# A late LayerNorm's transposes move into the next unit, and a stage's right operands are made over two units

## The chip, the cores and the metric

The kernel runs on one core of a Trainium2 chip. The metric is the device time of one execution in microseconds (us); the kernel before takes 1109.93 us (median of three runs, 1108.16 to 1110.4). TensorE's multiplications bound it; the other engines prepare their operands and take their results. Below, PE is TensorE, DVE is VectorE, ACT is ScalarE, POOL is GpSimd and SP is the engine that issues most of the DMAs.

## The reference, cut to what matters

2048 tokens of 512 features in fp32 pass through an RWKV-like block (attention part, then a channel mix) and a gated feed-forward block:

```
kk = (h * cm_mk + hh * (1 - cm_mk)) @ Wkey.T        # 512 -> 2048
kv = silu(kk) @ Wval.T                               # 2048 -> 512
sr = sigmoid((h * cm_mr + hh * (1 - cm_mr)) @ Wcr.T)
x  = x + sr * kv
...
x2 = x + attn(layernorm(x))
h  = layernorm(x2)                                   # the last norm
gate, up = split(h @ w_gate_up.T)                    # 512 -> 2 * 2048
out = x2 + (silu(gate) * up) @ w_down.T              # 2048 -> 512
```

h and hh are a normalised token and the one before it. The second norm of the channel mix and the last norm both stand between large products.

## The kernel before, in words

Every fp32 operand of a multiplication is split in two: a high part, rounded to the type in which PE multiplies at full rate (ACT copies it), and a low part, the rest (DVE or POOL subtracts). A product of two operands is three passes: high by high, high by low, low by high.

The last and longest part of the kernel is 48 **units** on PE; in the trace unit 8 begins at 423.3 us, unit 16 at 594.8, unit 32 at 850.2. Units 0 to 15 are key units (the channel mix), units 16 to 47 gate units (the feed-forward). The tokens are four blocks of 512; two blocks make a pair. There are four **stages**: units 0 to 7 (channel mix, first pair), 8 to 15 (channel mix, second pair), 16 to 31 (feed-forward, first pair), 32 to 47 (feed-forward, second pair). Inside a unit a 2x2 block product is made by a scheme with seven products in place of eight (Strassen-Winograd). Its seven left operands (A11 ... S4) come from the unit's weights; the seven right operands (B11, T3, T2, B21, T1, T4, B22) come from the tokens of the pair and are the same for all units of a stage. They lie in `combo`, one buffer for all stages, so an operand of the next stage may be written only after the last unit of the stage before has used it.

A unit on PE (`unit`, from L639): X A11·B11, V S3·T3, tiles of slot 0, Y S2·T2, X A12·B21, tiles of slot 1, Y S1·T1, tiles of slot 2, Z A22·T4, Y S4·B22, tiles of slot 3. X, Y, V and Z are four of the PSUM banks. Each product is six matmuls. The tiles (`out_tile`, six matmuls each) multiply the activated results of the unit before with the second weight matrix; they use the four other PSUM banks, A[0] to A[3], and DVE adds each to `resid` (L1215). A key unit has two tiles in each slot, a gate unit one, unit 17 only two in all.

All engines take their instructions in order, and this order is written out by hand in the function `unit` of each engine. DVE's chain in a unit: `accumulate` of slot 0, `seed` (Z from Y and the copied seventh product, L1266; PE's S1 product waits for it), `sums` (left operands of the next unit, L1161 to L1166, in the fresh units 0 to 7 and 16 to 31), slot 1, `sum_v` (L1270; PE's S4 product waits for it), slot 2, `gate` (L1280, gate units; PE's S3 product of the next unit waits for both), slot 3, and pieces of the last norm. ACT's: copy of X to Y (L890; PE's S2 product waits for it), copy of V (L896), high parts of the gated tiles of the unit before (L845), high parts of the next unit's left operands (L810, L813) and of the second weights (L823), and SiLU of the results as they come (L854, L866).

For the right operands of the next stage, the last unit of a stage has on DVE, in between: `combo_lo_of` (low parts, L1189, two instructions per operand), `make_t2` (L1196), `make_t4` (L1203), and on ACT `combo_hi_of` (high parts, L840, two per operand). T4 is made out of B21 and T2, T2 out of B22 and T1, and T1 and T3 by `right_sums` (L1180, L1183), some units ahead, in units 4, 14 and 30. In the kernel before, all high parts are issued in the last unit of the old stage, and of the low parts T4's and B22's in the first unit of the new one, behind `seed`.

The last norm of block j runs on DVE in seven pieces over some units. The last piece writes normalised tiles (L1241) at the end of unit `NORM3_UNIT[j]` (12, 13, 25 and 29). Right behind slot 3 of the same unit PE transposes them (16 small matmuls, L637) into A[0] to A[3], and ACT copies the four banks back (L879), after which the next unit's first tiles may write them. The copies must wait for all 16 transposes, since they write the buffer that the transposes read.

Of the kernel before, what the change touches and what calls it, by code (L numbers as in the profile page):

```python
# [32 lines left out]
BLOCKS = TOKENS // BT  # L33
# [55 lines left out]
B11, B21, B22, T4, T1, T2, T3 = range(SEVEN)  # L89
# [4 lines left out]
def stage_of(u):  # L94
    return max(n for n in range(STAGE_COUNT) if FIRST[n] <= u)


def stage_start(u):
    return u in FIRST
# [20 lines left out]
def tiles_until(u):  # L120

    if u < KEYS:
        return 2 * SUBS * u
    return SUBS * (u + KEYS - 1) - (LAG if u > KEYS else 0)
# [37 lines left out]
def piece_unit(j, piece):  # L162
    return piece_at(j, piece) // 2

NORM3_UNIT = tuple(piece_unit(j, NORM_PIECES - 1) for j in range(BLOCKS))
NORM3_AFTER = tuple(tiles_until(u) for u in NORM3_UNIT)

SUMS_UNIT = (None, 4, KEYS - 2, FIRST[3] - 2)  # L170

# [29 lines left out]
def build(nc, x, wts, wide, tall, vectors, identity, out):  # L201
# [3 lines left out]
    with ExitStack() as ctx:  # L205
# [270 lines left out]
        def _(pe):  # L476
# [6 lines left out]
            def product(acc, u, a, c, fresh):  # L483

                if stage_start(u):
                    pe.wait_ge(combo_lo, 2 * (SEVEN * stage_of(u) + MADE_ORDER.index(c) + 1))
                wts_of = left[u % 2]
                for k in range(2):
                    hi, lo = (wts_of[:, part, a, k * P:(k + 1) * P] for part in range(2))
                    pe.matmul(acc[:], hi, combo[:, c, k, 0, :], start=fresh and k == 0, stop=False, skip_group_check=True)  # L490
                    pe.matmul(acc[:], hi, combo[:, c, k, 1, :], start=False, stop=False, skip_group_check=True)  # L491
                    mm = pe.matmul(acc[:], lo, combo[:, c, k, 0, :], start=False, stop=k == 1, skip_group_check=True)  # L492
                return mm
# [137 lines left out]
            def norm3(j):  # L631
                pe.wait_ge(z3_ready, SUBS * (j + 1))
                for n in range(NORM3_AFTER[j], NORM3_AFTER[j] + SUBS):
                    s = n % SUBS
                    pe.wait_ge(added, n - SUBS + 1)
                    for k in range(KT):
                        mm = pe.transpose(A[s][:, k * P:(k + 1) * P], fin[j % 2][:, s, k * P:(k + 1) * P], ident[:])  # L637
                    mm.then_inc(t3_psum, 1)

            def unit(u):  # L640
                def some(slot):
                    for n in tiles_in(u, slot):
                        out_tile(n)

                def left_there(part):
                    if u in FRESH:
                        pe.wait_ge(left_lo, 2 * fresh_until(u) + part + 1)
                    else:
                        pe.wait_ge(left_loaded[u % 2][part], 16 * same_parity(CACHED, u))

                left_there(0)
                if u:
                    pe.wait_ge(silu_done, silu_by(u - 1, 0))
                else:
                    pe.wait_ge(sr_ready, SUBS * (BLOCKS - 1) + 1)
                product(X, u, A11, B11, True).then_inc(p1, 1)
                left_there(1)
                if u == 0:
                    pe.wait_ge(sr_ready, SUBS * (BLOCKS - 1) + 3)
                elif is_key(u - 1):  # L660
                    pe.wait_ge(silu_done, silu_by(u - 1, 2))
                else:
                    pe.wait_ge(gated, 2 * (u - KEYS))
                product(V, u, S3, T3, True).then_inc(p7, 1)
                some(0)
                pe.wait_ge(x_copied, u + 1)
                product(Y, u, S2, T2, False).then_inc(p6, 1)
                product(X, u, A12, B21, False).then_inc(p2, 1)
                some(1)
                pe.wait_ge(z_seeded, u + 1)  # L670
                product(Y, u, S1, T1, False).then_inc(p5, 1)
                some(2)
                product(Z, u, A22, T4, False).then_inc(p4, 1)
                pe.wait_ge(v_summed, u + 1)
                product(Y, u, S4, B22, False).then_inc(p3, 1)
                some(3)
                for j in range(BLOCKS):
                    if u == NORM3_UNIT[j]:
                        norm3(j)

            pe.wait_ge(ident_loaded, 16)
            first_norm1()
# [27 lines left out]
        def _(act):  # L710
# [157 lines left out]
            def gated_hi(u):  # L868
                for b in range(2):
                    n = 2 * (u - KEYS) + b  # L870
                    act.wait_ge(gated, n + 1)
                    inner_hi_tile(4 * KEYS + n, 2 * chunk_of(u) + b, u % 2)
# [9 lines left out]
            def unit(u):  # L882

                after = stage_of(u + 1) if u + 1 < UNITS and stage_start(u + 1) else None
                act.wait_ge(p1, u + 1)
                if u:
                    act.wait_ge(silu_done, silu_by(u - 1, 3 if is_key(u - 1) else 1))
                else:
                    act.wait_ge(sr_ready, SUBS * BLOCKS)
                act.activation(Y[:], X[:], ACT.Copy).then_inc(x_copied, 1)  # L890
                if after is not None:
                    combo_hi_of(after, B11)
                act.wait_ge(p7, u + 1)
                if u:
                    act.wait_ge(v_summed, u)
                act.activation(seventh[:], V[:], ACT.Copy).then_inc(seventh_copied, 1)  # L896
                if u > KEYS:
                    gated_hi(u - 1)
                if after is not None:
                    combo_hi_of(after, T3)  # L900
                if u + 1 in FRESH:
                    unit_left_hi(u + 1, 0)
                if is_key(u):
                    unit_right_hi(u)
                if after is not None:
                    combo_hi_of(after, T2)
                if u + 1 in FRESH:
                    unit_left_hi(u + 1, 1)
                act.wait_ge(p2, u + 1)
                if is_key(u):  # L910
                    key_tile(u, 0, X)
                else:
                    gate_tile(u, 0, X)
                    unit_right_hi(u)
                if after is not None:
                    combo_hi_of(after, B21)
                    combo_hi_of(after, T1)
                if is_key(u):
                    act.wait_ge(p4, u + 1)
                    key_tile(u, 1, Z)  # L920
                    act.wait_ge(v_summed, u + 1)
                    key_tile(u, 2, V)
                act.wait_ge(p3, u + 1)
                if is_key(u):
                    key_tile(u, 3, Y)
                else:
                    gate_tile(u, 1, Y)
                if after is not None:
                    combo_hi_of(after, T4)
                    combo_hi_of(after, B22)  # L930
                for j in range(BLOCKS):
                    if u == NORM3_UNIT[j]:
                        norm3(j)

            act.wait_ge(vec_loaded, 16)
            matrix_hi(ITEM_R)
# [46 lines left out]
        def _(dve):  # L983
# [298 lines left out]
            def unit(u):  # L1282

                after = stage_of(u + 1) if u + 1 < UNITS and stage_start(u + 1) else None
                def some(slot):
                    for n in tiles_in(u, slot):
                        accumulate(n)

                some(0)
                if after is not None:  # L1290
                    combo_lo_of(after, B11)
                seed(u)
                if stage_start(u) and u:
                    combo_lo_of(stage_of(u), T4)
                    combo_lo_of(stage_of(u), B22)
                if u + 1 in FRESH:
                    sums(u + 1)
                if is_key(u):
                    last_norm(u, 0)
                some(1)  # L1300
                if after is not None:
                    make_t2(after)
                sum_v(u)
                if after is not None:
                    combo_lo_of(after, T3)
                if u in SUMS_UNIT:
                    right_sums(SUMS_UNIT.index(u))
                some(2)
                if after is not None:
                    combo_lo_of(after, T2)  # L1310
                    combo_lo_of(after, B21)
                if not is_key(u):
                    gate(u, 0)
                    gate(u, 1)
                some(3)
                last_norm(u, 1)
                if after is not None:
                    make_t4(after)
                    combo_lo_of(after, T1)

            first_norm1()
            dve.wait_ge(const_done, 7)
# [232 lines left out]
```

## Time and profile before

| | |
|---|---|
| median of three runs | 1109.93 us (1108.16 to 1110.4) |
| the profiled execution's own time | 1111.04 us |
| its span, first to last instruction | 1109.2 us |
| mean granted TensorE clock | 0.989 of full speed |
| PE busy | 1065.0 us, 96% of the span |
| PE weight loads busy | 875.0 us, 79% |
| DVE busy | 641.9 us, 58% |
| ACT busy | 485.7 us, 44% |
| POOL busy | 542.1 us, 49% |

PE's busy time is made of matmul records that overlap: a matmul of 512 columns shows 0.39 us, and the next begins 0.23 us after the first one's start. Idle time on PE is therefore read from the distance of two starts, and from the bracket with which the timeline marks a wait. The granted clock has two levels, 1.2 GHz (shown as 0.50) and 2.4 GHz (1.00).

### The profile page before, as it was taken

Reading aid. Unit: us, or ns where it says so; the run is one execution under the profiler, and the core shown is the slowest. Engines: PE = TensorE matmul, PEld = TensorE weight load, DVE = VectorE, ACT = ScalarE, POOL = GpSimd, SP = SyncE. Lnnn points to the kernel's source line nnn. Section 1 sums busy time; section 2 is a strip of 40 time slices with the busy share of each in tenths; the row PEclk is TensorE's granted clock in tenths of the full one; section 3 lists DMA queues with packets and bytes.
Section 4 is the critical chain, followed back from the end, with each engine's and each line's share of the span. In section 5 each row is a group of like instructions: output and inputs, shape, how many; then the busy total and the mean of one; then the engine's idle time right before and its main releaser. Section 6 shows DMA issues by size and latency. Waiting matters only on the chain. (4 is left out here: it accounts for less than half of the span.)

```text
span 1109.2 us, 13090 instructions
## 1 busy us (share of the span) xinstructions
PE 1065.0 (96%) x4704; PEld 875.0 (79%) x4704; DVE 641.9 (58%) x1106; ACT 485.7 (44%) x807; POOL 542.1 (49%) x451
## 2 busy tenths in 40 slices
PE   5979999999999999999998999999998999999998
PEld 4758888777788887888786888887876888888887
DVE  7867756685355457465348567676668433333334
ACT  6765676856534435323344433334434222222221
POOL 6483552733766554544435555664554333333322
PEclk9989999999999999999998999999999999999999
DMA  8000222258834444553312466565436454444422
GB/s 306 1 1 1 38 39 76 39 209 255 322 125 150 145 171 122 190 160 109 128 62 105 165 231 192 198 220 190 171 114 218 133 191 141 152 144 150 151 77 76
DMA packets 45233, 157.18 MB, mean 142 GB/s; under 512 B 4080, under 2 KB 4208, under 8 KB 40560
## 3 DMA queue, kind: packets, MB, share of 16 engines
q1 hardware_dynamic: 30000, 108.10, 27.9%
q0 software_dynamic: 15168, 48.24, 14.5%
q8 instruction: 37, 0.61, 0.2%
q14 instruction: 28, 0.23, 0.1%
HBM read 97.60 MB, written 58.72 MB: 141 GB/s over the span
## 5 line engine op out<-in xcount | busy, mean ns | idle before, releaser
L1215 DVE TENSOR_TENSOR resid<-bank,resid 128x512 f32<-128x512 f32 x240 | 164.7, 689 | 244.6 <-PE bank L481 243.0
L490 PE MATMUL bank<-combo,left 128*128 128x512 f32 x672 | 265.1, 395 | 12.7 <-ACT bank L890 7.2
L1447 POOL TENSOR_TENSOR inner<-made,inner 128x512 fp32r<-128x512 f32 x128 | 167.0, 1326 | 220.0 <-ACT inner L845 220.0
L491 PE MATMUL bank<-combo,left 128*128 128x512 f32 x672 | 263.5, 392 | 0.0
L492 PE MATMUL bank<-combo,left 128*128 128x512 f32 x672 | 263.3, 392 | 0.0
L479 PE MATMUL bank<-right,inner 128*128 128x512 f32 x512 | 199.3, 389 | 0.0
L480 PE MATMUL bank<-right,inner 128*128 128x512 f32 x512 | 199.2, 389 | 0.0
L481 PE MATMUL bank<-right,inner 128*128 128x512 f32 x512 | 199.2, 389 | 0.0
L1425 POOL TENSOR_TENSOR left<-quart,left 128x512 fp32r<-128x512 f32 x96 | 116.2, 1232 | 104.8 <-ACT left L810 53.9
L490 PEld LDWEIGHTS bank<-combo,left 128*128 128x128 f32 x672 | 127.3, 190 | 42.7 <-ACT bank L890 8.5
L492 PEld LDWEIGHTS bank<-combo,left 128*128 128x128 f32 x672 | 127.4, 190 | 26.8
L491 PEld LDWEIGHTS bank<-combo,left 128*128 128x128 f32 x672 | 127.5, 190 | 26.1
L1442 POOL TENSOR_TENSOR right<-tall_staged,right 128x512 fp32r<-128x512 f32 x64 | 85.2, 1342 | 56.8 <-ACT right L823 56.8
L479 PEld LDWEIGHTS bank<-right,inner 128*128 128x128 f32 x512 | 96.2, 188 | 20.5 <-POOL inner L1447 0.4
L481 PEld LDWEIGHTS bank<-right,inner 128*128 128x128 f32 x512 | 96.1, 188 | 20.0
L480 PEld LDWEIGHTS bank<-right,inner 128*128 128x128 f32 x512 | 96.1, 188 | 19.9
L1404 POOL TENSOR_TENSOR operand<-made,operand 128x512 fp32r<-128x512 f32 x64 | 84.9, 1425 | 44.2 <-ACT operand L719 44.2
L866 ACT ACTIVATE made<-bank 128x512 f32<-128x512 f32 x64 | 37.9, 593 | 150.7 <-PE bank L492 150.7
L854 ACT ACTIVATE made<-bank 128x512 f32<-128x512 f32 x64 | 37.5, 586 | 95.2 <-PE bank L492 95.2
L845 ACT ACTIVATE inner<-made 128x512 fp32r<-128x512 f32 x128 | 77.2, 628 | 2.7 <-ACT made L854 0.4
L1280 DVE TENSOR_TENSOR made<-bank,made 128x512 f32<-128x512 f32 x64 | 44.0, 690 | 58.5 <-ACT made L866 37.1
L479 PE MATMUL bank<-operand,weights 128*128 128x512 f32 x176 | 69.3, 394 | 1.4 <-DVE made L1128 1.1
(128 smaller groups left out, 1461.7 us busy)
## 6 DMA issues: line engine op xcount, KB each, us to landing
kept_left<-left SPq DMA_DIRECT2D x24, 1792.0 KB, 8.2
left<-kept_left POOLq DMA_DIRECT2D x24, 1024.0 KB, 7.1
left<-kept_left POOLq DMA_DIRECT2D x24, 768.0 KB, 5.1
tall_staged<-tall SPq DMA_DIRECT2D x64, 256.0 KB, 3.6
quart<-wide SPq DMA_DIRECT2D x24, 512.0 KB, 4.2
raw<-kept SPq DMA_DIRECT2D x32, 256.0 KB, 6.3
landed<-wts SPq DMA_DIRECT2D x20, 256.0 KB, 5.8
resid<-x POOLq DMA_DIRECT2D x4, 1024.0 KB, 9.2
```

Source lines behind the costliest of these rows:

```text
L479: pe.matmul(acc, left(0), right(0), start=first, stop=False)
L480: pe.matmul(acc, left(0), right(1), start=False, stop=False)
L481: return pe.matmul(acc, left(1), right(0), start=False, stop=last)
L490: pe.matmul(acc[:], hi, combo[:, c, k, 0, :], start=fresh and k == 0, stop=False, skip_group_check=True)
L491: pe.matmul(acc[:], hi, combo[:, c, k, 1, :], start=False, stop=False, skip_group_check=True)
L492: mm = pe.matmul(acc[:], lo, combo[:, c, k, 0, :], start=False, stop=k == 1, skip_group_check=True)
L845: act.activation(inner[:, h % 4, i, 0, :], made_at(n), ACT.Copy).then_inc(inner_hi, 1)
L1215: dve.tensor_tensor(tile, A[s][:], tile, ALU.add).then_inc(added, 1)
L1404: pool.tensor_tensor(place(kind, b, k, 1), made[:, (n + k) % RING, :], place(kind, b, k, 0).bitcast(F32), ALU.subtract).then_inc(op_lo, 1)
L1425: lo = pool.tensor_tensor(left[u % 2][:, 1, a[0]:a[0] + n, :], quart[:, a[0] + 1:a[0] + 1 + n, :], left[u % 2][:, 0, a[0]:a[0] + n, :].bit ...
L1442: pool.tensor_tensor(right[:, g % 2, i, 1, :], tall_staged[i][:], right[:, g % 2, i, 0, :].bitcast(F32), ALU.subtract).then_inc(right_lo, 1)
L1447: pool.tensor_tensor(inner[:, h % 4, i, 1, :], made_at(n), inner[:, h % 4, i, 0, :].bitcast(F32), ALU.subtract).then_inc(inner_lo, 1)
```

## The change

Two things. First, `NORM3_UNIT` is one unit later (13, 14, 26, 30), and the transposes stand inside that unit, between the products A12·B21 and the tiles of slot 1; `NORM3_AFTER` is the first tile of slot 1, and that tile now waits for the first of ACT's copies. ACT's copies stand behind the copy of V and the gated high parts, ahead of the left operands.

Second, the order of the right operands' work. On DVE `seed` goes ahead of B11's low parts, `sum_v` ahead of `make_t2`; T1's low parts and `make_t4` go to the beginning of the new stage's first unit, ahead of slot 0; B22's low parts go behind `sum_v`; `right_sums` goes from slot 2 to behind slot 3 and the gates. On ACT T4's and B22's high parts go into the first unit of the new stage, behind the copy of V, and T2's goes behind the first SiLU.

```diff
-NORM3_UNIT = tuple(piece_unit(j, NORM_PIECES - 1) for j in range(BLOCKS))
-NORM3_AFTER = tuple(tiles_until(u) for u in NORM3_UNIT)
+NORM3_UNIT = tuple(piece_unit(j, NORM_PIECES - 1) + 1 for j in range(BLOCKS))
+NORM3_AFTER = tuple(tiles_in(u, 1)[0] for u in NORM3_UNIT)
...PE
                 product(X, u, A12, B21, False).then_inc(p2, 1)
+                for j in range(BLOCKS):
+                    if u == NORM3_UNIT[j]:
+                        norm3(j)
                 some(1)
...
                 some(3)
-                for j in range(BLOCKS):
-                    if u == NORM3_UNIT[j]:
-                        norm3(j)
...ACT
                 if u > KEYS:
                     gated_hi(u - 1)
+                for j in range(BLOCKS):
+                    if u == NORM3_UNIT[j]:
+                        norm3(j)
+                if stage_start(u) and u:
+                    combo_hi_of(stage_of(u), T4)
+                    combo_hi_of(stage_of(u), B22)
                 if after is not None:
                     combo_hi_of(after, T3)
...
-                if after is not None:
-                    combo_hi_of(after, T2)
...
                 if after is not None:
+                    combo_hi_of(after, T2)
                     combo_hi_of(after, B21)
                     combo_hi_of(after, T1)
...
-                if after is not None:
-                    combo_hi_of(after, T4)
-                    combo_hi_of(after, B22)
-                for j in range(BLOCKS):
-                    if u == NORM3_UNIT[j]:
-                        norm3(j)
...DVE
+                if stage_start(u) and u:
+                    combo_lo_of(stage_of(u), T1)
+                    make_t4(stage_of(u))
                 some(0)
-                if after is not None:
-                    combo_lo_of(after, B11)
                 seed(u)
                 if stage_start(u) and u:
                     combo_lo_of(stage_of(u), T4)
-                    combo_lo_of(stage_of(u), B22)
+                if after is not None:
+                    combo_lo_of(after, B11)
                 if u + 1 in FRESH:
                     sums(u + 1)
                 if is_key(u):
                     last_norm(u, 0)
                 some(1)
+                sum_v(u)
+                if stage_start(u) and u:
+                    combo_lo_of(stage_of(u), B22)
                 if after is not None:
                     make_t2(after)
-                sum_v(u)
-                if after is not None:
                     combo_lo_of(after, T3)
-                if u in SUMS_UNIT:
-                    right_sums(SUMS_UNIT.index(u))
                 some(2)
-                if after is not None:
-                    combo_lo_of(after, T2)
-                    combo_lo_of(after, B21)
                 if not is_key(u):
                     gate(u, 0)
                     gate(u, 1)
+                if after is not None:
+                    combo_lo_of(after, T2)
                 some(3)
+                if u in SUMS_UNIT:
+                    right_sums(SUMS_UNIT.index(u))
                 last_norm(u, 1)
                 if after is not None:
-                    make_t4(after)
-                    combo_lo_of(after, T1)
+                    combo_lo_of(after, B21)
```

## Rows read from the trace of the kernel before

**Rows 1.** The page's first part: busy us, share of the span, instructions.
```profile
PE 1065.0 (96%) x4704; PEld 875.0 (79%) x4704; DVE 641.9 (58%) x1106; ACT 485.7 (44%) x807; POOL 542.1 (49%) x451
```
**Rows 2.** Waits of PE: line waited for, us in total, times, longest.
```profile
PE bank L490 <- ACT bank L890: 7.2, 3, 5.1
PE bank L637 <- DVE raw L1241: 5.4, 3, 2.0
```
**Rows 3.** PE's timeline at last norms' transposes: start, us, engine, line, operation, [idle <-releaser].
```profile
550.59 2.56 PE L637 MATMUL bank<-ident,raw 128*128 128x128 f32 x16 [2.03 <-DVE raw L1241]
552.80 0.78 PE L490 MATMUL bank<-combo,left 128*128 128x512 f32 x1
...
815.76 1.97 PE L637 MATMUL bank<-ident,raw 128*128 128x128 f32 x16 [1.70 <-DVE raw L1241]
```
**Rows 4.** Behind block 0's transposes: PE's next product, ACT's four copies.
```profile
527.87 0.47 PE L490 MATMUL bank<-combo,left 128*128 128x512 f32 x1
...
528.15 2.07 ACT L879 ACTIVATE raw<-bank 128x512 f32<-128x512 f32 x4 [2.27 <-PE bank L637]
```
**Rows 5.** Windows: length, busy us of PE, PEld, DVE, ACT, POOL; PEclk, DMA, GB/s.
```profile
551.80:555.20 3.40, 3.40 (x13) 2.92 (x12) 0.00 (x0) 2.01 (x4) 0.00 (x0) 0.50 1.12 389
...
599.40:603.00 3.60, 0.01 (x1) 0.00 (x0) 3.60 (x6) 1.19 (x3) 1.77 (x2) 1.00 0.80 336
603.00:609.80 6.80, 5.27 (x12) 4.13 (x13) 2.82 (x5) 2.72 (x5) 1.97 (x2) 0.50 0.00 0
...
750.00:753.20 3.20, 1.51 (x12) 1.08 (x11) 3.13 (x6) 0.00 (x0) 0.07 (x1) 1.00 0.95 330
```
**Rows 6.** PE's timeline at the starts of units 8 and 16.
```profile
429.49 0.50 PE L490 MATMUL bank<-combo,left 128*128 128x512 f32 x1 [0.59 <-ACT bank L890]
...
596.20 0.44 PE L490 MATMUL bank<-combo,left 128*128 128x512 f32 x1
...
599.02 0.39 PE L481 MATMUL bank<-right,inner 128*128 128x512 f32 x1
604.53 0.79 PE L490 MATMUL bank<-combo,left 128*128 128x512 f32 x1 [5.13 <-ACT bank L890]
...
615.06 0.39 PE L492 MATMUL bank<-combo,left 128*128 128x512 f32 x1
615.29 0.39 PE L490 MATMUL bank<-combo,left 128*128 128x512 f32 x1
```
**Rows 7.** PE's timeline in units 31 and 32.
```profile
836.16 0.47 PE L490 MATMUL bank<-combo,left 128*128 128x512 f32 x1 [2.07 <-DVE made L1280]
...
852.39 0.47 PE L490 MATMUL bank<-combo,left 128*128 128x512 f32 x1 [0.70 <-issue]
...
856.91 0.50 PE L490 MATMUL bank<-combo,left 128*128 128x512 f32 x1 [1.53 <-ACT bank L890]
```
**Rows 8.** DVE's timeline in units 15, 16 and 30.
```profile
586.19 0.42 DVE L1166 TENSOR_TENSOR quart<-quart 128x256 f32<-128x256 f32 x1
...
591.94 6.32 DVE L1189 TENSOR_TENSOR combo<-raw,combo 128x512 fp32r<-128x512 f32 x4
...
608.11 2.48 DVE L1189 TENSOR_TENSOR combo<-raw,combo 128x512 fp32r<-128x512 f32 x4
...
830.74 3.47 DVE L1183 TENSOR_TENSOR raw<-raw,raw 128x512 f32<-128x512 f32 x2
...
834.74 1.27 DVE L1280 TENSOR_TENSOR made<-bank,made 128x512 f32<-128x512 f32 x2
```
**Rows 9.** POOL's timeline in unit 15.
```profile
594.25 6.92 POOL L1447 TENSOR_TENSOR inner<-made,inner 128x512 fp32r<-128x512 f32 x4
```
**Rows 10.** ACT's timeline in units 15 and 16: SiLU of V, T4's and B22's high parts.
```profile
595.49 0.58 ACT L854 ACTIVATE made<-bank 128x512 f32<-128x512 f32 x1
...
601.81 2.19 ACT L840 ACTIVATE combo<-raw 128x512 fp32r<-128x512 f32 x4 [3.92 <-DVE raw L1203]
603.91 0.57 ACT L890 ACTIVATE bank<-bank 128x512 f32<-128x512 f32 x1
```

## The prediction

> **What bounds the kernel now.** First the page's busy shares: PE is busy for 96% of the span [rows 1], so a change can only win what PE stands idle or runs slow for, and lose by adding to it. Then PE's waits, longest first [rows 2]: 7.2 us in three places for ACT's copy of X (L890), 5.4 us in three for the last norm's tiles (L1241). Then PE's own timeline at those places [rows 3, 6, 7] and the windows for the granted clock [rows 5]. The reader is to see that nearly all of it lies where this change works: behind units 12, 25 and 29 (only three of four blocks wait), and at the starts of the stages. Two of the places also cost clock: after the first it is 1.2 GHz for 3.4 us, after the second for 6.8 us [rows 5], while a wait of 1.7 us at 750 and one at 815 cost none [rows 3, 5]. No row shows another cause.
>
> **Yardsticks.** Two full-speed matmuls start 0.23 us apart (615.06 and 615.29 [rows 6]), a group of six takes 1.36 us. A DVE subtraction of 512 columns with both inputs in SBUF comes every 0.60 us while POOL rests (four in 2.48 us at 608.11), but every 1.6 to 1.8 us while POOL has its own queue of them (four in 6.32 us) [rows 8]; POOL's then take 1.7 us each [rows 9], near 1.25 alone. So they alternate, one POOL instruction (about 1.2 us) to one of DVE. An ACT high part comes every 0.54 us (four in 2.19 [rows 10]).
>
> A rule on this pair: the Trainium skill, "SBUF — State Buffer", section "SBUF: two separate sides", calls the port pair that the two share an exclusive lock, held for the whole instruction. The trace agrees (1.58 us against 0.62 for one [rows 8]). It speaks against this change, which puts more such DVE work in a row; by a shared bandwidth instead, each side would be a little slower and step C below would come out some 3 us better.
>
> **A. The last norm's transposes.** Removed: PE's waits for L1241. At block 1 the idle time is 2.03 us in the bracket and 2.2 from the last tile's normal end, at blocks 2 and 3 1.7 in the bracket, 1.85 by the starts [rows 3]; block 0 waits for nothing. Sum 5.9. In the new place z is written a whole 8 us before PE reaches it (two products, a slot, two products), and the banks' last tiles are long added. Also removed: the slow clock at 551.8. In its 3.4 us PE does the work of 1.7 [rows 5], so 1.7 us. Idle time before transposes is what preceded it, and blocks 2 and 3 with 1.7 us show none; I take it as gone.
> Added: tile 1 of slot 1 now stands directly behind the transposes and waits for ACT's first copy. At block 0 PE's next product began at 527.87, ACT's first copy at 528.15 and takes about 0.6 [rows 4]; a tile would have begun at 528.8, so 0.9 us of idle time. ACT needs all 16 transposes, later copies come every 0.49 us against 1.36 per tile and hide. Four blocks: 4 x 0.85 = 3.4. The transposes themselves (16 x 0.11) stay on the path either way. What is queued behind the wait on ACT: left and right high parts and the first SiLU; POOL's low parts and DVE's gates depend on them. In gate unit 26 or 30 they end about 17 us after the unit's start, the next unit asks for the second part at 19. SP's next loads of weights hang on these low parts, and have a unit's length: hidden. If that 2 us were gone, unit 27 or 31 would begin late by the rest.
> A: -5.9 - 1.7 + 3.4 = -4.2. Bounds: each added wait from 0.6 (the copy alone) to 1.8 us (with all four copies' 2.07 less what a tile covers); with or without 1.7 of clock: -5.2 to +1.3.
>
> **B. Start of unit 8.** ACT's copy of X no longer stands behind four high parts of T4 and B22 that wait for `make_t4`. The 0.6 us in the bracket, 0.75 by the starts [rows 6], goes. DVE's chain in unit 8 (T1, `make_t4`, two additions) ends at about 429.9, PE needs `seed` only at 434: key units have four tiles between. B: -0.75, bounds -0.9 to +1.
>
> **C. Start of unit 16.** Before, PE's last tile matmul started at 599.02 and S2·T2 at 604.53; with the slow clock S4·B22 began at 615.29 [rows 6], where at full speed without a wait it would be at 607.1 (598.9 plus six groups). So 8.2 us are lost there. Now the chain anew, in the old trace's time:
> 1. In unit 15 PE's S2 lies 14 groups before the 598.9 of unit 16, at 579.9 to 581.4; `seed` waits for it, B11 goes behind, and the sums, which ended at 586.6 [rows 8], end at 587.4. ACT then makes the left operand's second part at once, so POOL's two left parts and an inner part (3 x 1.2) fall among DVE's `sum_v`, `make_t2` and T3: two additions end at 588.6, then 0.7 + 4 x 0.6 + 3 x 1.2 is 595.3, less 0.6 of POOL's first that `sum_v` covers: T3 done near 594.7, T2 made at 592.3.
> 2. ACT: six high parts from 592.3 to 595.5, two SiLUs with a high part between, SiLU of V done 597.3 (before 596.07 [rows 10]). V S3·T3, before at 596.20, waits 1.15.
> 3. DVE from 594.7: eight subtractions (T2, B21, T1, T4) and four additions by 0.6, one more for slot 0, `seed` 0.7, two POOL inner parts in between 2.4: 605.6. PE is ready for S1 at 603.0 + 1.15: waits 1.5.
> 4. DVE from 605.6: T4 1.2, sums 1.6, addition 0.6, `sum_v` 0.7, B22 1.2, POOL's left parts of unit 17 in between 3.3: 614.2. PE is ready for S4 at 605.6 + 3 x 1.36 = 609.7: waits 4.5.
> Sum of waits 7.1, against 8.2. A wait of 4.5 us is of the kind before which the clock fell (5.1 us at 599.4), so I add one slow stretch, 1.7. C: -8.2 + 7.1 + 1.7 = +0.6. Bounds: POOL in nobody's way, waits 2.5 and no slow clock: -5.7; one more POOL instruction in steps 1 to 4 each and 6.8 us of slow clock: +6.
>
> **D. Units 31 and 32.** Removed: S3 of unit 31 waited 2.07 (2.2 by the starts) for the gates of unit 30, which `right_sums` held up till 834.2 [rows 7, 8]; it is now behind them. S3 and S2 of unit 32 waited 0.70 and 1.53 [rows 7], 0.9 and 1.7 by the starts; small gaps between add 0.4. Sum 5.2. Added by the chain of step 3, for unit 31 with its start as zero: T2 made at 11.6, ACT's three operands till 14.9, last SiLU 15.5, gate 16.2 (V needs it at 16.3, no wait), T2 and B21 19.2; T1 and `make_t4` meet POOL's two inner parts, 2.4 + 2.4 = 24.0; addition and `seed` 25.2. PE is ready for S1 at 23.1: waits 2.1. B22 comes 0.5 late. D: -5.2 + 2.6 = -2.6, bounds -5.2 (POOL later than the chain) to +0.5.
>
> **Sum.** -4.2 - 0.75 + 0.6 - 2.6 = -7.0. The profiled execution took 1111.04 us, so 1104.0; it was 1.1 us above the median of the runs, 1109.93, and from that it is 1103.0, 0.6% less.
>
> **Rivals.**
> R1, unit 16 goes well: POOL's instructions fall beside additions (which read PSUM and aren't held up), waits 2.5, no slow clock. -4.2 - 0.75 - 5.7 - 2.6: 1096.7. For it: additions read PSUM, where POOL has no operand, and there are five of them in steps 3 and 4. Against: POOL's left parts are released by the very sums that precede B22.
> R2, the transposes bring the clock down at each block: a wait of 0.85 and 1.7 us of small matmuls, four times 1.7 us, and the loss at 551.8 stays: 6.8 more than A: 1109.8, no change. For it: 551.8 came with transposes. Against: 750 and 815 had more idle time beside the same transposes, and no fall.
> R3, slower: DVE's chain holds up `seed` at the first unit of each stage. Its place is L1189 and L1203 ahead of slot 0, its price 1.58 against 0.62 us for each subtraction if POOL is busy throughout [rows 8]. Units 15 and 16 have 14 more of them on the way to S1 and B22: 14 x 1.0 less the 8.1 counted (7 POOL instructions) is 5.9, and a second slow stretch 1.7; units 31 and 32 10 x 1.0 less 2.4 is 7.6: 15.2 more than forecast, 1118. It decides against the change from a total of 7 us, that is if POOL stays busy for half of these. Against: POOL's instructions are countable, four inner parts, three or four left parts.
> R4, the moves do nothing for PE since another wait ends at the same time (the gate of V in unit 16 or 31, a left part in 27 or 31): A's 3.4 added and C, D at zero: 1107.
>
> **How the numbers follow.** Forecast 0.62, R1 0.13, R2 0.07, R3 0.08, R4 0.10. The forecast's own range is 1100 to 1106. The range reaches down to 1097, the upper part of R1, and 1109, which takes in R4 and part of R2. Within 0.2% (2.2 us, what can be told from no change) lie R2 and a part of the forecast's upper end: 0.09; slower 0.07; faster 0.84.
>
> **What would show it.** After: L637 without an idle bracket for L1241, and behind each transposes group a bracket of 0.6 to 0.9 us for ACT L879; no L1280 wait in unit 31; L890 no longer among PE's waits at stage starts, L1266 (`seed`) and L1189 in its place, together 6 to 8 us around unit 16; at most one slow stretch there and none at the transposes. I am wrong if B22's wait in unit 16 is under 2 or over 7 us, if a first copy costs PE over 1.5 us, or if left parts (L1425) are waited for in units 27 or 31.

## The result, and the profile after

The changed kernel takes 1101.55 us (median of four runs, 1100.64 to 1101.63) against 1109.99 us of the kernel before: a ratio of 0.9925 with a 95% interval of 0.9908 to 0.9942, 8.4 us less. The forecast was 1103.0 and faster. The profiled execution took 1100.64 us, its span 1098.8.

The first part and PE's waits of the page after (the waits' columns are the line that waited, what released it, us in total, times, longest):

```profile
PE 1060.4 (97%) x4704; PEld 871.4 (79%) x4704; DVE 633.2 (58%) x1106; ACT 485.9 (44%) x807; POOL 537.9 (49%) x451
```
```profile
PE bank L491 <- ACT made L855: 3.3, 2, 2.6
PE bank L491 <- DVE combo L1189: 3.1, 2, 2.8
...
PE bank L480 <- ACT raw L880: 2.7, 4, 0.7
...
PE bank L491 <- DVE bank L1266: 2.5, 2, 1.7
```

Lines of PE's, ACT's and POOL's code are one higher than before, DVE's are the same. The waits of [rows 2] are gone: none for L1241, and none for ACT's copy of X. In their place stand four short waits for ACT's copies behind the transposes (L880), and waits for `seed` (L1266) and for B22's low parts (L1189), as the last part of the prediction listed them; the line for L855 (before: L854) stands at 278 to 281 us, far ahead of unit 8, in work that the change doesn't touch. The wait for V in unit 16 is put down to `issue`, 0.33 us in the bracket, 0.5 by the starts.

PE's timeline after, behind block 0's transposes and at the waits of units 16 and 32 (start us, us, engine, line, operation, [idle <-releaser]):

```profile
533.66 0.82 PE L638 MATMUL bank<-ident,raw 128*128 128x128 f32 x6
535.17 0.50 PE L480 MATMUL bank<-right,inner 128*128 128x512 f32 x1 [0.69 <-ACT raw L880]
...
592.95 0.47 PE L491 MATMUL bank<-combo,left 128*128 128x512 f32 x1 [0.33 <-issue]
...
600.86 0.50 PE L491 MATMUL bank<-combo,left 128*128 128x512 f32 x1 [0.83 <-DVE bank L1266]
...
604.89 0.39 PE L493 MATMUL bank<-combo,left 128*128 128x512 f32 x1
608.05 0.77 PE L491 MATMUL bank<-combo,left 128*128 128x512 f32 x1 [2.78 <-DVE combo L1189]
...
849.98 0.50 PE L491 MATMUL bank<-combo,left 128*128 128x512 f32 x1 [1.70 <-DVE bank L1266]
```

The tile at 535.17 is the price of the new place, once per block; the answers to [rows 6, 7] are the other five lines. The clock after the longest wait, by windows (length, busy us of PE, PEld, DVE, ACT, POOL, granted clock, DMA share, GB/s):

```profile
603.00:607.70 4.70, 2.28 (x10) 1.53 (x9) 4.67 (x6) 2.06 (x3) 4.14 (x4) 1.00 0.00 0
607.70:611.10 3.40, 3.04 (x7) 2.48 (x8) 1.41 (x3) 0.11 (x1) 2.58 (x2) 0.50 0.24 57
```

From unit 8 on, one slow stretch of 3.4 us is left in this execution where there were 3.4 and 6.8 [rows 5].

### The profile page after: what moved, and what is told of

Same layout as the page of the kernel before. It is cut to its first block, busy times and chain, and to the rows that moved or that the text cites. A ratio compares the mean times of both kernels' runs of the same rounds, so it can differ in the third digit from the quotient of the medians.

```text
span 1098.8 us, 13090 instructions
## 1 busy us (share of the span) xinstructions
PE 1060.4 (97%) x4704; PEld 871.4 (79%) x4704; DVE 633.2 (58%) x1106; ACT 485.9 (44%) x807; POOL 537.9 (49%) x451
## 4 chain that ended last, share of the span: by engine, by line
PE 83%; DVE 8%; ACT 3%; POOL 3%; issue 1%; DMA 1%; SPq 0%; ACTq 0%; DVEq 0%
PE bank L480 15%; PE bank L481 14%; PE bank L482 14%; PE bank L491 13%; PE bank L492 13%; PE bank L493 13%; DVE combo L1189 2%; POOL operand L1405 1%; POOL weights L1393 1%; DVE made L1080 1%; DVE weights L1107 1%; DMA tall_staged<-tall 1%; PE bank L638 1%; DVE resid L1215 1%; PE bank L548 0%
## 5 line engine op out<-in xcount | busy, mean ns | idle before, releaser
L1443 POOL TENSOR_TENSOR right<-tall_staged,right 128x512 fp32r<-128x512 f32 x64 | 82.8, 1303 | 67.4 <-ACT right L824 67.4
L855 ACT ACTIVATE made<-bank 128x512 f32<-128x512 f32 x64 | 37.6, 587 | 83.8 <-PE bank L493 83.8
```

The costliest lines, as they stand in the source:

```text
L1443: pool.tensor_tensor(right[:, g % 2, i, 1, :], tall_staged[i][:], right[:, g % 2, i, 0, :].bitcast(F32), ALU.subtract).then_inc(right_lo, 1)
```

## The experiments

All are timed against the kernel before, in the same session.

### One part at a time

a_only is the kernel before with the first part of the change, r_only the changed kernel with the first part undone:

```diff
 # a_only, against the kernel before
-NORM3_UNIT = tuple(piece_unit(j, NORM_PIECES - 1) for j in range(BLOCKS))
+NORM3_UNIT = tuple(piece_unit(j, NORM_PIECES - 1) + 1 for j in range(BLOCKS))
 ... and norm3(j) moved on PE and ACT; the right operands as before
 # r_only, against the changed kernel
-NORM3_UNIT = tuple(piece_unit(j, NORM_PIECES - 1) + 1 for j in range(BLOCKS))
+NORM3_UNIT = tuple(piece_unit(j, NORM_PIECES - 1) for j in range(BLOCKS))
 ... and norm3(j) moved back on PE and ACT
```

> The kernel before with the first part of the change alone (the last norm's transposes and copies inside the next unit). My theory: 5.9 us of waits for L1241 and the slow clock at the first of them (1.7) go, four waits of 0.85 us for ACT's first copy come: 4.2 us less, 1105.8; the waits at the starts of units 16 and 32 stay (5.1 and 1.5 us for L890). The rival, the small matmuls beside a short wait bring the clock down at each block: 1110 or more, with a granted clock of 0.5 beside L637. A second rival, what is saved here is only what the later stage starts wait for anyway: under 2 us.

> The second part alone (order of the right operands; the transposes stay behind slot 3). My theory: the rest of the gain, 4.2 us, 1105.8, and no overlap between the parts: PE's waits for L1241 stay at 5.4 us, in unit 16 its waits for L1270 or L1189, L1266 and L855 sum to 4.5 us as in the changed kernel. The rival, the parts need each other (the right sums behind slot 3 collide with the last norm's tiles in unit 14 or 29): the two single gains sum to less than 6 us.

a_only: 1107.83 us (ten runs) against 1110.22, ratio 0.998 (0.9971 to 0.999), 2.4 us less where 4.2 were expected. r_only: 1104.48 against 1110.22, ratio 0.9948 (0.9934 to 0.9963), 5.7 less where 4.2 were expected. The sum, 8.1, is the whole (8.4) within what the intervals leave open; neither needs the other. In r_only's trace the waits for L1241 stay at 5.4 us and those of unit 16 make 4.5 by the starts, as expected. In a_only's trace all four transposes look as they do after the whole change:

```profile
PE bank L490 <- ACT bank L890: 7.2, 3, 5.1
...
PE bank L479 <- ACT raw L879: 2.7, 4, 0.7
```

so the idle time did what was said: 5.9 us away and four times 0.73 by the starts (0.84 with the slower first matmul), 2.5 us net, and that is the measured gain. What did not come is the clock. The slow stretch at 551.8 is gone, but its trace has one behind the wait in unit 31, which stands in the kernel before too [rows 7] and cost no clock there:

```profile
830.20:833.00 2.80, 0.81 (x4) 0.46 (x3) 2.78 (x5) 1.63 (x3) 1.26 (x2) 1.00 1.11 410
833.10:836.50 3.40, 3.40 (x10) 2.63 (x9) 0.00 (x0) 1.52 (x3) 0.31 (x1) 0.50 0.98 311
```

The first window is the wait, the second the slow stretch. The second rival, that the stage starts behind would take back the gain, isn't excluded by the time, whose interval is 1.1 to 3.2 us, but by the trace: PE waits there 5.12, 0.98 and 1.51 us in the brackets, against 5.13, 0.70 and 1.53 [rows 6, 7], 0.25 us more in all. The windows of the kernel before at that wait have 1.00 in both:

```profile
833.70:836.20 2.50, 0.43 (x3) 0.07 (x1) 2.50 (x5) 1.63 (x3) 1.40 (x2) 1.00 1.08 413
836.20:839.60 3.40, 3.40 (x15) 2.80 (x16) 0.81 (x2) 1.77 (x4) 0.57 (x1) 1.00 0.93 279
```

### The right sums back to their place

```diff
                     combo_lo_of(after, T3)
+                if u in SUMS_UNIT:
+                    right_sums(SUMS_UNIT.index(u))
                 some(2)
 ...
-                if u in SUMS_UNIT:
-                    right_sums(SUMS_UNIT.index(u))
                 last_norm(u, 1)
```

> The changed kernel with right_sums back ahead of slot 2 in units 4, 14 and 30. My theory: unit 30's gates are late again and S3 of unit 31 waits about 2 us for L1280, while the wait of 1.7 us for seed in unit 32 stays: 2 us more than the changed kernel, 1103.5. The rival, that wait in the kernel before came from the transposes ahead of unit 30 and not from the sums: no wait, 1101.6.

1103.37 us against 1110.22, 1.8 more than the changed kernel. PE's waits have the line of [rows 7] again, and seed's are as in the changed kernel:

```profile
PE bank L491 <- DVE bank L1266: 2.5, 2, 1.7
...
PE bank L491 <- DVE made L1280: 2.0, 1, 2.0
```

That term of step D is shown. The medians of the two stand in different sessions, each with its own kernel before (ratios 0.9942 and 0.9925); the line in the trace decides, not the 1.8 us.

### POOL out of the way

```diff
 # unit_left_lo
+                w = 8 if u in (KEYS, KEYS + 1) else HALF
 ... and [..., :w] on its three operands
 # inner_lo_tile
+                w = 8 if 4 * (KEYS - 1) <= n < 4 * KEYS else BT
 ... and [..., :w] on its three operands
```

> The changed kernel, but POOL's low parts of the left operands of units 16 and 17 and of the inner tiles of unit 15 are computed for 8 columns of each block only; the rest of these parts stays what was there, so the output is not the reference's. Nothing else changes. My theory, what is left at the start of unit 16 is DVE's chain with POOL's instructions in between: the waits for L855 (0.5), L1266 (1.0) and L1189 (2.9) fall together from 4.4 to under 2 us, and the subtractions in units 15 and 16 come every 0.60 us: 3 us less than the changed kernel, 1098.5. The rival, the number of DVE's and ACT's own instructions sets it: waits as in the changed kernel within 0.5 us.

1094.67 us (two runs) against 1109.88, ratio 0.9864 (0.9845 to 0.9884): about 7 us less than the changed kernel, over twice what was expected. DVE's timeline of the changed kernel, from `make_t2` on:

```profile
584.88 3.00 DVE L1196 TENSOR_TENSOR raw<-raw 128x512 f32<-128x512 f32 x2
587.81 2.39 DVE L1189 TENSOR_TENSOR combo<-extra,combo 128x512 fp32r<-128x512 f32 x2
...
593.72 4.68 DVE L1189 TENSOR_TENSOR combo<-raw,combo 128x512 fp32r<-128x512 f32 x4
...
605.56 2.35 DVE L1189 TENSOR_TENSOR combo<-raw,combo 128x512 fp32r<-128x512 f32 x2
```

and the same instructions of pool_small:

```profile
583.89 1.29 DVE L1196 TENSOR_TENSOR raw<-raw 128x512 f32<-128x512 f32 x2
585.10 1.28 DVE L1189 TENSOR_TENSOR combo<-extra,combo 128x512 fp32r<-128x512 f32 x2
...
592.05 2.50 DVE L1189 TENSOR_TENSOR combo<-raw,combo 128x512 fp32r<-128x512 f32 x4
...
601.57 1.31 DVE L1189 TENSOR_TENSOR combo<-raw,combo 128x512 fp32r<-128x512 f32 x2
```

Between them DVE now stands idle for PE. The expectation named L855 for the wait of V; it is the `issue` line, which is gone as well. All three waits of unit 16 are gone, while those of unit 32, where POOL was left alone, stay:

```profile
PE bank L491 <- DVE bank L1266: 1.7, 1, 1.7
...
PE bank L491 <- DVE combo L1189: 0.3, 1, 0.3
```

So it is the alternation of the two engines, not the count of DVE's or ACT's own instructions, that holds PE in unit 16. The rival is out. The rule of the Trainium skill ("SBUF — State Buffer", "SBUF: two separate sides") that the two hold their shared port pair for a whole instruction agrees: 0.60 us from one subtraction to the next with POOL's instructions short, 1.2 to 1.7 for those that are held up with them long. This run changes only how long POOL's instructions are, so it does not tell a lock from a shared bandwidth. By PE's starts the waits were 4.4 us and the slow stretch behind them 1.5 (its matmuls stand 0.43 apart), 5.9 of the 7; the rest is within what single executions differ.

### Seed ahead of make_t4

```diff
                 if stage_start(u) and u:
                     combo_lo_of(stage_of(u), T1)
-                    make_t4(stage_of(u))
                 some(0)
                 seed(u)
                 if stage_start(u) and u:
+                    make_t4(stage_of(u))
                     combo_lo_of(stage_of(u), T4)
```

> The changed kernel with make_t4 behind seed in the first unit of each stage (T1 stays ahead). My theory, DVE's chain up to B22 is one chain: the waits for seed (L1266, 1.0 and 1.7 us) go, and B22's in units 16 and 32 grow by nearly as much, since the same instructions stand ahead of it: within 1 us of the changed kernel, 1101. The rival, each wait is its own cost: 2.7 us less, 1098.8.

1102.16 us against 1109.88, ratio 0.9932 (0.9917 to 0.9948), no gain. The waits for L1266 have gone and one line has taken them over:

```profile
PE bank L491 <- DVE combo L1189: 6.1, 3, 3.9
```

3.1 and 2.5 us before this edit, 6.1 after it, of which 0.2 in unit 8: the chain up to B22 is one chain, and this exchange inside it is worth nothing.

### The sums behind sum_v

```diff
                     combo_lo_of(stage_of(u), T4)
+                    combo_lo_of(stage_of(u), B22)
 ...
-                if u + 1 in FRESH:
+                if u + 1 in FRESH and u != KEYS:
                     sums(u + 1)
 ...
                 sum_v(u)
-                if stage_start(u) and u:
-                    combo_lo_of(stage_of(u), B22)
+                if u == KEYS:
+                    sums(u + 1)
```

> The changed kernel with B22's low parts directly behind T4's in the first unit of a stage, and in unit 16 the sums for unit 17 behind sum_v. Nothing is removed; the sums are only taken out of the way of S4. My theory: the wait for L1189 (2.9 us) in unit 16 goes, with it the risk of a slow stretch; ACT's second left part and the first SiLU of unit 16 come later, which gives back up to 1.5 us at the start of unit 17; unit 32 gains 0.5: 1099. The rival, unit 17 waits for its left part (POOL) as long as S4 waited before: 1101.6.

1096.86 us against 1109.88, ratio 0.9887 (0.987 to 0.9903), 4.2 less than the changed kernel by the ratios, where 2.5 were expected: in the trace the wait of 2.9 us went and the slow stretch behind it too (1.5). DVE's timeline shows B22 now directly behind T4, before POOL has its next parts (four in 2.48 us, no alternation), and `sum_v` at 603.21 ahead of the four sums:

```profile
600.20 2.48 DVE L1189 TENSOR_TENSOR combo<-raw,combo 128x512 fp32r<-128x512 f32 x4
602.61 0.68 DVE L1215 TENSOR_TENSOR resid<-bank,resid 128x512 f32<-128x512 f32 x1
603.21 0.68 DVE L1270 TENSOR_TENSOR bank<-bank,e 128x512 f32<-128x512 f32 x1
603.80 0.41 DVE L1161 TENSOR_TENSOR quart<-quart 128x256 f32<-128x256 f32 x1
```

L1189 is no longer among PE's waits; what comes back is 0.4 us for a left part in unit 17:

```profile
PE bank L491 <- POOL left L1427: 0.4, 1, 0.4
```

### The transposes one product earlier, and both

```diff
                 product(Y, u, S2, T2, False).then_inc(p6, 1)
-                product(X, u, A12, B21, False).then_inc(p2, 1)
                 for j in range(BLOCKS):
                     if u == NORM3_UNIT[j]:
                         norm3(j)
+                product(X, u, A12, B21, False).then_inc(p2, 1)
                 some(1)
```

> The changed kernel with the transposes between S2 and A12 in place of behind A12, so that one product (1.36 us) lies between the last transpose and the tile that waits for ACT's first copy. My theory, the remaining cost of the part is this one latency: the four waits of 0.7 us for L880 go, 3.3 us less by the starts, 1098.3. The rival, the additions of slot 0 or ACT's queue are late at the earlier place, and PE waits there instead: no gain or a loss.

> The transposes ahead of A12 and the sums behind sum_v together. Both theories right and separate: 3.5 to 4 us from the first, 2.5 from the second, 1095.5. The rival, one hides the other: 1097.8, as the first alone.

norm_early: 1097.8 us against 1110.22, ratio 0.9894 (0.9877 to 0.991), 3.4 less than the changed kernel by the ratios. The transposes are followed by A12 at once, and the tile behind it starts without a bracket:

```profile
531.01 1.91 PE L638 MATMUL bank<-ident,raw 128*128 128x128 f32 x16
532.68 0.48 PE L491 MATMUL bank<-combo,left 128*128 128x512 f32 x1
...
533.91 0.39 PE L493 MATMUL bank<-combo,left 128*128 128x512 f32 x1
534.13 0.39 PE L480 MATMUL bank<-right,inner 128*128 128x512 f32 x1
```

early_late: 1093.36 us against 1109.88, ratio 0.9851 (0.9837 to 0.9866). The expected 1095.5 was 2 us too high; the two are separate (8.2 less than the changed kernel by the ratios, 3.4 and 4.2 alone).

### T2 between the gates

```diff
 # against early_late
                     gate(u, 0)
+                if after is not None:
+                    combo_lo_of(after, T2)
+                if not is_key(u):
                     gate(u, 1)
-                if after is not None:
-                    combo_lo_of(after, T2)
```

> As early_late, and in unit 31 T2's low parts stand between DVE's two gates in place of behind both, where DVE stood idle for 1.4 us for ACT's last SiLU. My theory, the wait for seed in unit 32 (L1266, 1.7 us) is the end of one chain on DVE, so 1.2 us less ahead of it is 1.2 us less of wait: 1092.2. The rival, POOL's two inner parts then fall elsewhere into the chain and the wait stays: 1093.4.

1091.16 us (five runs, 1090.75 to 1092.29) against 1108.98, ratio 0.9841 (0.9828 to 0.9854). In the trace the wait of 1.7 us in unit 32 is gone, 0.9 in unit 16 stays; and the four subtractions of B21 and T1 now end before POOL's two inner parts begin (837.11), so they no longer alternate (2.49 us where early_late had 3.58):

```profile
834.65 2.49 DVE L1189 TENSOR_TENSOR combo<-raw,combo 128x512 fp32r<-128x512 f32 x4
```

That rules the rival out. By time the step is not told from early_late: 1.1 us by the ratios (0.9841 against 0.9851), with intervals that overlap; the rest of the distance of the two medians lies between their sessions, whose kernels before differ by 0.9. This and early_late are the fastest versions, 9.3 and 8.2 us below the changed kernel by the ratios.

## Why the prediction was right

The direction, the places and the mechanism held, and the sum was 7.0 where 8.4 were measured. Two of its four terms were mis-sized, in opposite directions, so that the sum is nearer than its terms; that part is luck. Between the two profiled executions, by the starts of the same products, 10.4 us are gone, about: A 3.9, B 0.9, C 2.0, D 2.8, and 0.9 ahead of unit 8, in work that the change doesn't touch.

**A, the transposes: -4.2 forecast, -2.4 in a_only (1.1 to 3.2 by its interval).** The waits for L1241 went and four of 0.69 us in the bracket came, as worked out (0.85 forecast, 0.73 to 0.84 by the starts). No left part was late in units 27 and 31. The part of the step that failed is "I take it as gone", the 1.7 us of clock. In the profiled execution of the changed kernel it is gone (A is 3.9 there), in a_only's trace another stretch stands behind the wait in unit 31; over the runs it gives nothing back: by the ratios the changed kernel lies 2.5 us below r_only, which has everything but this part, and a_only 2.4 below the kernel before, as much as the idle time alone. In r_only, where the transposes are back behind slot 3, the clock is 0.5 again from 550.0 to 553.4, at block 1's. Whether another stretch comes in each of a_only's ten runs the traces can't say; their mean granted clock, 0.989 to 0.991, is not above that of the kernel before, 0.989 to 0.993. Why the clock falls behind one such wait and not behind the next stays open.

**B, unit 8: -0.75 forecast, -0.9 between the two profiles.** No gap over 0.26 us between two starts is left there. It was not tried alone.

**C, unit 16: +0.6 forecast, -2.0 in the profiled execution (-8.2 + 4.4 of waits + 0.3 of slower first matmuls behind them + 1.5 of clock).** This is the term that was mis-sized most, and the reason why 8.4 us came and not 7.0. The three waits were found at the places and behind the instructions that steps 2 to 4 name, each shorter: 0.5 us for V against 1.15, 1.0 for `seed` against 1.5, 2.9 for B22 against 4.5; 4.4 against 7.1 in sum. With the offset between the two traces (V·T3 due at 596.20 in the one, 592.46 in the other, 3.7 us) the chain reads: T2 made 591.6 (forecast 592.3), SiLU of V 596.6 (597.3), `seed` done 604.5 (605.6), B22 done 611.6 (614.2). Over half of the error is in step 4, from `seed` to B22 7.1 us against 8.6: 3.3 us of POOL's left parts of unit 17 were counted in between, and the trace has one of them at the last sum and one at B22. The slow stretch of 1.7 came in this execution (1.5 by the starts), not in others of the same wait, below. One of the signs was missed with it: L1266 and L1189 were to come to 6 to 8 us around unit 16 and show 3.6 in the brackets.

**D, units 31 and 32: -2.6 forecast, -2.8 by the starts.** S3 waits for no gate; 1.70 us for `seed` (2.1 forecast) and 0.3 in the bracket for B22, 0.47 by the starts (0.5 forecast). sums_back shows the first term.

R1, unit 16 going well, lies on the side to which C erred, but the forecast is nearer: waits of 4.4 us and a slow stretch, against its 2.5 and none, and 7.1 and one in the forecast. POOL's instructions did alternate with the subtractions. What it says of the additions is so: two of them took 1.28 us, 0.60 from one to the next, beside a busy POOL.

```profile
592.52 1.28 DVE L1215 TENSOR_TENSOR resid<-bank,resid 128x512 f32<-128x512 f32 x2
592.44 4.80 POOL L1448 TENSOR_TENSOR inner<-made,inner 128x512 fp32r<-128x512 f32 x3 [3.40 <-ACT inner L846]
```

R2, the clock falling at each block's transposes, is refuted: in the changed kernel's trace it is 1.00 from 400 us up to the wait for B22 in unit 16, and behind it again through the transposes of blocks 2 and 3. R3's chain is real, but POOL comes in between six or seven times, not throughout; its 8.1 us of counted POOL instructions are 8.7 by the forecast's own terms (3.0, 2.4 and 3.3), which changes nothing. R4 found nothing, and its 1107 does not follow from its terms: with C and D at zero, A and B leave 1105.0.

The reading under "What bounds the kernel now" is wrong in one point. The list of waits, longest first, leaves out two that are as long:

```profile
PE bank L555 <- DVE resid L1050: 10.1, 3, 9.4
...
PE bank L479 <- ACT held L747: 5.7, 1, 5.7
```

They lie in the first 80 us, ahead of the units, 9.4 of the first before PE has any work. So it isn't true that nearly all of PE's waiting lies where this change works: of some 40 us in the list of the kernel before, 15.4 do (7.2, 5.4, 2.1 and 0.7). No term of the sum uses that sentence.

## What to carry to other kernels

A wait for an engine's short copy is hidden by putting one independent product between producer and consumer: order the bound engine so that something lies behind each hand-over, not only ahead of it. In a chain whose end is what the bound engine waits for, an exchange of two members ahead of that end is worth nothing (seed_first), but taking out what the bound engine doesn't wait for is worth all of it (sums_late), and filling the time in which the chain's engine stands idle took away a whole wait in the trace (t2_between). Price such a chain instruction by instruction, and treat the other engine's instructions as separate items, which fall in between only when they are released.

## What the runs showed of the hardware

A wait of PE of the same length may or may not bring the slow clock. The wait for B22 in unit 16 is 2.9 to 3.0 us in the changed kernel, r_only, sums_back and norm_early; the granted clock fell behind it only in the first. Windows of sums_back, the last tile before, the wait, and what follows:

```profile
602.50:605.90 3.40, 3.40 (x16) 2.81 (x15) 3.37 (x6) 1.55 (x3) 2.13 (x2) 1.00 0.00 0
605.90:609.10 3.20, 0.42 (x2) 0.00 (x1) 3.20 (x5) 1.71 (x3) 2.63 (x3) 1.00 0.00 0
609.10:612.50 3.40, 3.37 (x15) 2.81 (x16) 2.10 (x4) 0.60 (x1) 2.29 (x2) 1.00 0.37 67
```

The wait of 2.1 us in unit 31 did the reverse, no fall in the kernel before, a fall in a_only, and none in sums_back. Nor is it a matter of the edits: PE waits 2.1 us for L1140 at 230 us in every trace, in work that no edit touches, and the clock falls behind it in three of the eleven (before, seed_first, early_late). Windows from 230.6 us on, of the kernel before and of the changed one:

```profile
230.60:234.00 3.40, 3.40 (x10) 2.64 (x9) 3.37 (x7) 0.00 (x0) 0.00 (x0) 0.55 1.00 408
```
```profile
230.60:234.00 3.40, 3.40 (x16) 2.79 (x15) 3.37 (x6) 0.58 (x1) 0.00 (x0) 1.00 0.99 395
```

In all eleven traces together, from 60 us on and by the brackets: no fall behind waits of up to 1.9 us, a fall behind 6 of 16 waits of 2.0 to 2.1 us and behind 5 of 13 of 2.5 to 2.8, and a fall behind each that was longer (3.95 in seed_first, 5.1 in before and a_only, 5.7 for L747 or L748 in all). So a term for the clock belongs in the range of a forecast and not in its sum, unless the wait is far longer. Second, shortening twelve of POOL's instructions (pool_small) moved PE by some 7 us, though none of the waits that went was for an instruction of POOL.
